# One more weight chunk left behind the first stage, weight rounding begun one unit later, one more unit with a split second half

## The reference, cut to what matters

```python
# x: (32, 128, 2048) fp32; per batch b a session weight W[b] (128, 256) is gathered
h   = gelu(einsum('bct,bch->bht', x * channel_mask, W) + b_sess)        # 256 hidden rows
o   = (einsum('bht,hs->bst', h, W2) + b2) * time_mask                    # 128 rows, 2048 columns
w_q = fp8_e4m3(weight * 448 / max|weight|)                               # weight: 2048 x 2048
o_q = fp8_e5m2(o * 57344 / max|o|)                                       # max over all batches
out = x + (o_q @ w_q.T) / scales + bias
```

## Time and profile before

| what | value |
|---|---|
| median of three runs | 836.15 us |
| the profiled execution | 836.48 us, its span 834.7 us |
| PE busy | 822.0 us (98%) |
| DVE, ACT, POOL busy | 484.3, 337.0, 508.0 us |
| PE in the chain that ended last | 94% |
| last matmul of stage one ends at | 383.6 us |

### The profile page before, as it was taken

The page is one execution under the profiler, slowest core; times in us unless marked ns, Lnnn a source line. Parts: engine busy times, 40 slices in busy tenths (PEclk is TensorE's granted clock), DMA queues, the critical chain, the costliest instruction groups (busy, mean ns, idle before and its releaser), DMA issues.

```text
span 834.7 us, 10103 instructions
## 1 busy us (share of the span) xinstructions
PE 822.0 (98%) x3517; PEld 480.8 (58%) x3564; DVE 484.3 (58%) x503; ACT 337.0 (40%) x352; POOL 508.0 (61%) x230
## 2 busy tenths in 40 slices
PE   9899999999999999999999999999999999999998
PEld 6588888777767676765444444444444444444444
DVE  6989999888888888888552323232332323232322
ACT  7689999988898889883200000000000000000000
POOL 3599999989999999995983242424242424242322
PEclk9999999999999999999999999999999999999999
DMA  7989999878867777656974767676768686868682
GB/s 272 370 294 338 326 335 339 326 282 313 303 265 297 300 296 277 253 207 230 361 239 123 255 235 264 226 266 224 275 215 281 209 284 212 284 212 283 213 253 106
DMA packets 75008, 222.08 MB, mean 266 GB/s; under 512 B 37594, under 2 KB 39650, under 8 KB 55778
## 3 DMA queue, kind: packets, MB, share of 16 engines
q1 hardware_dynamic: 74080, 220.62, 75.0%
q10 hardware_dynamic: 898, 1.09, 0.4%
HBM read 144.35 MB, written 69.21 MB: 256 GB/s over the span
## 4 chain that ended last, share of the span: by engine, by line
PE 94%; DMA 2%; DVE 1%; issue 1%; ACT 0%; SPq 0%; DVEq 0%
PE ps_h L1050 51%; PE ps_h L959 20%; PE ps_o L974 11%; PE ps_o L990 8%; PE ps_o L986 4%; DMA more<-more 1%; DMA x_sb<-in_x 0%; DVE hl L737 0%; DMA wt<-in_L_cond_W_sess 0%; PE ps_h L1026 0%; PE ps_o L1050 0%; DVE more L845 0%; DVE o_and_max L747 0%; DVE o_max L752 0%; DMA sid_i<-in_itok_B 0%
## 5 line engine op out<-in xcount | busy, mean ns | idle before, releaser
L1050 PE MATMUL ps_h<-wqT,x_sb 128*128 128x512 bf16 x1877 | 411.3, 378 | 2.4 <-ACT x_sb L684 0.2
L1050 PEld LDWEIGHTS ps_h<-wqT,x_sb 128*128 128x128 fp8e5 x1920 | 187.7, 98 | 224.4 <-ACT x_sb L684 0.3
L516 POOL TENSOR_TENSOR xl<-x_sb,xh 128x1024 fp32r<-128x1024 f32 x62 | 149.6, 2412 | 17.9 <-ACT xh L596 17.9
L959 PE MATMUL ps_h<-xh,whl 128*128 128x512 f32 x508 | 150.7, 417 | 3.8 <-DVE hl L737 3.8
L559 POOL TENSOR_TENSOR x_sb<-x_sb,bias_sb 128x2048 f32<-128x2048 f32 (+1 forms) x15 | 66.7, 4445 | 132.8 <-DMA x_sb<-in_x 132.8
L559 POOL TENSOR_TENSOR h<-h,bias_sb 128x2048 f32<-128x2048 f32 (+1 forms) x15 | 66.7, 4443 | 122.6 <-DMA h<-in_x 122.6
L865 DVE SCALAR_TENSOR_TENSOR o_and_max<-ps_h,scales,h 128x512 f32<-128x512 f32 (+1 forms) x59 | 44.0, 746 | 136.2 <-PE ps_h L1050 136.2
L865 DVE SCALAR_TENSOR_TENSOR o_and_max<-ps_h,scales,x_sb 128x512 f32<-128x512 f32 x59 | 44.2, 750 | 134.3 <-PE ps_h L1050 134.3
L959 PEld LDWEIGHTS ps_h<-xh,whl 128*128 128x128 f32 x508 | 95.1, 188 | 42.7 <-issue 21.9
L747 DVE SCALAR_TENSOR_TENSOR o_and_max<-ps_o,b_sb,steps 128x1024 f32<-128x1024 f32 (+1 forms) x65 | 82.1, 1264 | 28.7 <-PE ps_o L990 27.8
L737 DVE TENSOR_TENSOR hl<-ps_h,hh 128x1024 fp32r<-128x1024 f32 x63 | 76.8, 1219 | 11.1 <-ACT ps_h L603 11.0
(11 more groups left out here) (100 smaller groups left out, 653.1 us busy)
## 6 DMA issues: line engine op xcount, KB each, us to landing
x_sb<-in_x SPq DMA_DIRECT2D x44, 1024.0 KB, 7.0
masked_out<-o_and_max SPq DMA_DIRECT2D x32, 1024.0 KB, 5.5
o_in<-masked_out SPq DMA_DIRECT2D x32, 1024.0 KB, 8.9
out<-o_and_max SPq DMA_DIRECT2D x27, 1024.0 KB, 5.1
wqT<-in_L_ffn_weight SPq DMA_DIRECT2D x23, 684.0 KB, 9.8
wt<-in_L_ffn_weight SPq DMA_DIRECT2D x40, 384.0 KB, 5.4
h<-in_x SPq DMA_DIRECT2D x14, 1024.0 KB, 7.1
wraw<-split_w SPq DMA_DIRECT2D x28, 256.0 KB, 6.1
```

Source lines behind the costliest of these rows:

```text
L516: pool.tensor_tensor(xl[:, u % 2, :], x_cols(u), xh[:, u % 2, :].bitcast(fp32), ALU.subtract)\
L959: mm = nc.tensor.matmul(to[:, cols], whl[:, b % DIRECT, rows], xs[:, u % 2, cols], start=(k == 0), stop=(k == 2))
L1050: mm = nc.tensor.matmul(bank, q[:, k // 2, :, k % 2], wq[:, n, k, cols], start=(k == 0), stop=(k == KT - 1))
```

## The change

Unit 27 joins the units whose second half is split. Rounding begins one unit later (QUANT = 27, EARLY_CHUNKS = 34), so chunks 34 to 42 are `late`, nine in place of eight. DVE's `exponents` and `round_at` of chunk 34 stay in stage one, moved behind `split_h_rest` in turn 61 and into turn 62, and POOL rounds the chunk behind bias 0. ACT scales chunks 0 to 35 in stage one, before 0 to 36. DVE no longer has a `round_at` ahead of `quantize` of batch 1, and has four chunks (35 to 38) in place of three (36 to 38) between the output scale and the first eviction. SP loads one chunk fewer and ACT's queue one more.

```diff
-    SPLIT_H1 = [u for u in range(4, 27)]
+    SPLIT_H1 = [u for u in range(4, 28)]
...
-    QUANT = SCANS + 2
+    QUANT = SCANS + 3
...
# gpsimd, behind add_bias(x2[0]), add_bias(x2[1]), add_bias(x2_more[0]):
-            for i in late[0:2]:
+            for i in late[0:3]:
...
-            for i in late[2:6]:
+            for i in late[3:7]:
...
-            for i in late[6:]:
+            for i in late[7:]:
...
# vector, turn u of stage one:
+                if 0 <= u - QUANT - 1 < EARLY_CHUNKS:
+                    exponents(u - QUANT - 1)
                 if 0 <= u - QUANT - 1 < EARLY_CHUNKS + 1:
-                    exponents(u - QUANT - 1)
-                if 0 <= u - QUANT - 1 < EARLY_CHUNKS:
                     round_at(u - QUANT - 1)
                 if u + 1 < UNITS:
                     split_h_rest(u + 1)
+                if u - QUANT - 1 == EARLY_CHUNKS - 1:
+                    exponents(EARLY_CHUNKS)
...
# vector, behind stage one:
             late = range(EARLY_CHUNKS, CHUNKS)
-            round_at(late[0])
             quantize(1, 1, True, slice(0, T))
...
-            for i in late[1:4]:
+            for i in late[1:5]:
                 exponents(i)
                 round_at(i)
...
-                if y in CHUNK_BEHIND and 4 + CHUNK_BEHIND.index(y) < len(late):
-                    i = late[4 + CHUNK_BEHIND.index(y)]
+                if y in CHUNK_BEHIND and 5 + CHUNK_BEHIND.index(y) < len(late):
+                    i = late[5 + CHUNK_BEHIND.index(y)]
```

## The result

The changed kernel takes 839.73 us by the median (838.56 to 842.87) against 836.15: a ratio of 1.0036, 95% interval 1.0022 to 1.005, or 1.8 to 4.2 us slower. Its profiled execution had a span of 839.7 us, 5.0 above that of before. Executions of one kernel differ by 3 to 4 us. In the profiled ones of this document the first product of stage two begins anywhere from 385.98 to 389.78 us, though none shows a wait of PE between 60 us and the end of stage one: that spread comes from the first 60 us.

What follows compares the result with a forecast made beforehand. PE, busy 98% of the span, was taken as the bound. Unit 27's -0.34 plus 3.0 for the later burst gave +2.66 us on the profiled 836.48, 839.1, or 838.8 by the median; range 835.3 to 841.2.

Steps and rivals of the forecast that it cites:

- Unit 27: Stage one, unit 27: six split matmuls take 1.38 us instead of 1.72, other engines in time; -0.34 us.
- the rival on unit 27: Unit 27: POOL's second subtraction comes late and PE gets back its 0.34 us as a gap; 839.1, chance 0.03.
- Rest of stage one: Stage one's other turns: chunks run one unit later at no cost; 0, bounds -0.05 and +0.2 us.
- The chain of chunks: Behind stage one, ACT, DVE, POOL: chunks 35 to 38 delay the first eviction 3.66 us; 1.0 us PE gap at y = 4.
- The first transpose: Batch 2's transpose, wanted at y = 6: issued 406.53 instead of 402.87, lands about 410, no gap (bounds 0 and 0.7).
- The burst and the second transpose: 4.2 MB of DMA ahead of batch 3's transpose shifts 3.0 us (1.2 to 3.66), starting y = 9 at 423.6.
- POOL's late bias 3: Stage two: POOL 3 us late, y = 9 evicted at 434.4; y = 13 wants the bank at 437.4, nothing more lost.
- The shared port pair: VectorE and GpSimd lock: `quantize` clear of a POOL pass could win 1.0 us; by the rows the overlap stays.
- the five: Chances: forecast 0.55, burst hardly moves 0.14, faster 0.13, stretched 0.15, unit 27 fails 0.03.
- the burst hardly moves: Rival, stage two: DMA is saturated anyway, only y = 4's gap or one chunk counts; +0.7 to +0.9, 837.0, chance 0.14.
- Faster: Rival: y = 0 evicted before 402.6, batch 3's transpose lands at 420.4, only unit 27's gain left; 835.8, chance 0.13.
- Everything stretches: Rival: POOL passes meet DVE's fast operations, first eviction at 404.5 or later, burst 5 us late; +5, 841.2, chance 0.15.

Runs made afterwards that it cites:

- the kernel with chunk 38 moved: Changed kernel with chunk 38 passing DVE behind the eviction of y = 3 instead of ahead of the first eviction: 838.05 us, ratio 0.9998.
- The delay experiment: Kernel before with three unused 128x1024 reductions on VectorE put ahead of the first eviction: 838.58 us, ratio 1.0016.
- SP's order: SP's 2 MB of x issued behind the transpose of batch 3: on the changed kernel 837.83 us, ratio 1.0004; on the kernel before 835.85 us, 0.9982.
- chunks alone: Changed kernel with unit 27 left unsplit, so only the chunks move: 841.52 us, ratio 1.0047.
- quantizing early: Changed kernel with DVE quantizing batch 2 before it waits for chunk 38: 841.17 us, ratio 1.0039.
- The fill experiment: Changed kernel with 12 more matmuls, results overwritten, ahead of TensorE's wait for the transpose of batch 3: 841.36 us, ratio 1.0037.

## Why the prediction was right

- **Unit 27**: -0.34 forecast, -0.33 measured, and the experiment with it alone shows no gap in stage one. POOL and ACT were in time. L987 has six matmuls more and L991 four fewer, so the rival on unit 27 did not occur.
- **Rest of stage one**: 0 forecast. From unit 28's `project1` to the end of stage one's last matmul it took 205.0 us (178.29 to 383.33), before 205.1 (178.43 to 383.56).
- **The chain of chunks**: the first eviction forecast at 402.80, less unit 27's 0.34; it began at 402.61. Scaling of 37 and 38 forecast at 395.8 and 400.4, measured 395.61 and 400.19. The gap at y = 4: 1.0 forecast, 1.18 measured. That this chain is the cause, and not unit 27, the two halves of the change show; that it acts through DVE's order, the kernel with chunk 38 moved shows.
- **The first transpose**: forecast issue 406.53, less the same 0.34, measured 406.34; no gap at y = 6, as taken. It landed 3.1 us behind its issue.
- **The burst and the second transpose**: a shift of 3.0 was taken between 1.2 and 3.66. Measured from the first product it is 3.58, near the upper bound. The prediction held following the issue (3.66) and the bytes of one more chunk (1.2) against each other and took a value between. The delay experiment shows parts that add: 2.3 from the eviction, 1.3 from the chunks' order, give or take 0.3. That bytes land it, SP's order shows: 5.6 us in place of 11.5.
- **POOL's late bias 3**: taken as no loss at y = 13. None is seen there in the changed kernel, but only because PE itself was late; with chunk 38 moved the same lateness costs 1.28 us.
- **What was not in the sum**: the clock. The forecast of 838.8 sits 0.9 us below the median of 839.7. The profiled execution has 1.65 us for it, behind 3 us of idle. Of the nine executions, the two with a mean clock of 1.0 took 838.56 and 839.04, the four at 0.996 took 839.73 to 842.87. A mean clock doesn't say where a fall lies: both profiled executions, before and after, have one in their first 40 us too (at 32 to 36 us and at 8 to 12), so that one fall reads 0.998 and two read 0.996. Two terms were thus too small: the shift of the burst (3.0, measured 3.58) and "a gap of PE costs its own length", which put the clock at nothing. The forecast landed in its range since the first is small and the second does not strike every execution.
- **The shared port pair**: the overlap that I let stand stayed, with `quantize` at 2.31 us and POOL's pass at 2.50 us. The small product behind `quantize` of batch 1 (L856, now L857) fell from 1.41 to 0.16 us: before, it ran beside a POOL pass of 2.61 us that began at 389.03, now POOL is idle until 391.27. Both agree with the exclusive lock that the Trainium skill (SBUF — State Buffer, two separate sides) describes.
- **The chances**: the five add up to 1.00, so the 0.02 kept for a time below 832 belongs to no case.
- **The rivals**: "the burst hardly moves" failed at its own mark (a transpose landing at 421 or before; it was 423.8). "Faster" failed at its mark, chunk 38 scaled before 399.9; it was 400.19. "Everything stretches" did not occur: POOL kept its durations.

## What to carry to other kernels

Where a chain of links through several engines runs beside the bounding one, ask at a change of its count which link now falls behind a busy stretch of an engine. Here one scaling slipped from before ACT's widenings to behind them, and the first eviction came 3.7 us later. Work on that chain should stand behind what the bounding engine waits for, in every queue: DVE's evictions ahead of chunk 38, SP's transpose ahead of x that is not needed yet. And look at SP's order whenever a small transfer lands late in a saturated stretch; it was worth 1.5 us here by the ratio, 0.9 inside the profiled execution, even before the change.

## What the runs showed of the hardware that I had not expected

A gap of TensorE can cost more than its length. Behind idle gaps of 2.99 us (y = 9, changed kernel), 3.2 us (chunks alone) and 2.08 us (y = 4, quantizing early) the granted clock went to its lower level, 1.2 GHz, for 3.4 us, which cost some 1.65 us each. Behind gaps of 2.02, 1.95, 1.28, 1.18 and 0.76 us in stage two it stayed at 2.4 GHz. The fill experiment kept it there through a wait of the same transpose.

This must not be read as a limit near 2.05 us. Stage one of the same traces goes against it. Timeline of PE in the kernel before, and its busy time by stretch:
```profile
31.96 1.41 PE L959 MATMUL ps_h<-xh,whl 128*128 128x512 f32 x4 [1.87 <-DVE hl L737]
```
```profile
32.00:36.00 4.00, 4.00 (x11) 3.21 (x12) 3.71 (x3) 1.74 (x2) 0.92 (x1) 0.59 0.99 323
```
The same two views of the changed kernel:
```profile
33.68 1.15 PE L960 MATMUL ps_h<-xh,whl 128*128 128x512 f32 x4 [2.53 <-DVE hl L737]
```
```profile
33.00:37.00 4.00, 3.32 (x15) 2.76 (x16) 3.96 (x4) 1.68 (x2) 0.95 (x1) 1.00 1.01 370
```
A gap of 1.87 us was followed by the fall, one of 2.53 us was not. So the length of a gap alone does not tell whether the clock falls, and what else decides it these runs don't show. Each of these is one profiled execution, and the two changed-kernel executions with a mean clock of 1.0 had no fall at all, so not every execution falls at y = 9.
